# Causal zeroing on GpSimd instead of mask products on TensorE, with a retimed schedule, in an attention-and-mixture kernel

## The reference

```python
x = x + xattn(layernorm(x), ctx, ctx)        # 16 query heads, 4 key/value heads, width 32
    q, k = rope(rms_norm(q) ), rope(rms_norm(k))
    scores = q . k / sqrt(32); scores[key later than query] = -1e30
    out = softmax(scores) @ v @ w_out.T
x = x + ffn(layernorm(x))
    probs = softmax(x @ w_router); top 4 of 128 experts, weights normalised
    basis = silu(x @ w_gate[k]) * (x @ w_up[k])          # 8 shared bases of width 256
    out = sum over chosen experts of mix[expert] . basis @ w_down + shared expert
```

## Time and profile before

| | |
|---|---|
| median of 3 runs | 868.03 us (867.49 to 869.01) |
| the profiled execution | 869.35 us, its span 866.6 us |
| PE busy | 800.5 us, 92% |
| DVE, ACT, POOL busy | 650.2, 574.9, 493.8 us |

### The profile page before, as it was taken

One profiled execution on the slowest core, in us unless ns is written; L12 is line 12 of the kernel. 1 busy time (PEld: TensorE's weight loads), 2 busy tenths in 40 slices (PEclk: granted clock), 3 DMA queues, 4 the chain that ended last, 5 costly groups with the idle time before them and its releaser, 6 DMA issues.

```text
span 866.6 us, 15361 instructions
## 1 busy us (share of the span) xinstructions
PE 800.5 (92%) x4264; PEld 617.3 (71%) x4264; DVE 650.2 (75%) x1627; ACT 574.9 (66%) x1412; POOL 493.8 (57%) x682
## 2 busy tenths in 40 slices
PE   2668799999999999989999889989999999999998
PEld 1446567677776777768777668767777777877876
DVE  4736777788886767887888686878878875788774
ACT  1657877687776666778777575767787765554542
POOL 5457537894269526796278634797255512762461
PEclk9965999999999999999999999999999999999999
DMA  8031234544554245645445344454454443553650
GB/s 300 30 98 40 82 95 146 175 139 131 171 173 157 87 158 177 211 150 168 148 155 169 119 159 154 147 176 129 144 175 157 141 138 131 194 175 132 206 194 25
DMA packets 57795, 126.76 MB, mean 146 GB/s; under 512 B 12048, under 2 KB 28784, under 8 KB 57712
## 3 DMA queue, kind: packets, MB, share of 16 engines
q1 hardware_dynamic: 55888, 121.84, 42.8%
q10 hardware_dynamic: 1824, 3.94, 1.2%
HBM read 107.16 MB, written 4.19 MB: 128 GB/s over the span
## 4 chain that ended last, share of the span: by engine, by line
PE 67%; POOL 9%; DVE 6%; issue 6%; SPq 5%; ACT 3%; DMA 2%; POOLq 0%; DVEq 0%; ACTq 0%
PE u L1455 41%; PE u L1476 7%; PE o_bank L1371 3%; PE s L1331 3%; PE pair L1355 3%; SPq L557 2%; PE u L1439 2%; SPq L547 2%; POOL r_b L715 2%; DVE w_l L1102 1%; PE pair L1358 1%; POOL w_l L753 1%; PE s L1391 1%; DMA w_raw<-in_shared_w_down 1%; DMA w_raw<-in_w_units 1%
## 5 line engine op out<-in xcount | busy, mean ns | idle before, releaser
L1455 PE MATMUL u<-w_h,t_h 128*128 128x512 f32 x640 | 265.9, 415 | 8.4 <-POOL w_l L753 5.0
L1455 PE MATMUL u<-w_h,t_l 128*128 128x512 f32 x640 | 250.9, 392 | 0.0
L1455 PE MATMUL u<-w_l,t_h 128*128 128x512 f32 x640 | 250.8, 392 | 0.0
L1102 DVE TENSOR_TENSOR w_l<-w_raw,w_h 128x512 fp32r<-128x512 f32 x288 | 240.9, 864 | 0.0
L792 ACT ACTIVATE w_h<-w_raw 128x512 fp32r<-128x512 f32 x384 | 219.3, 622 | 27.1 <-DMA w_raw<-in_w_units 21.8
L753 POOL TENSOR_TENSOR w_l<-w_raw,w_h 128x512 fp32r<-128x512 f32 x96 | 135.4, 1410 | 101.5 <-ACT w_h L792 101.0
L827 ACT ACTIVATE scores<-scores,mx 128x384 f32<-128x384 f32 (+1 forms) x224 | 128.6, 575 | 62.0 <-DVE mx L1047 61.0
L1047 DVE CUSTOM_DVE_ANT_0 scores<-s,mask_qk 128x384 f32<-128x384 f32 (+1 forms) x224 | 112.5, 504 | 60.3 <-PE s L1331 59.4
L1455 PEld LDWEIGHTS u<-w_h,t_h 128*128 128x128 f32 x640 | 121.4, 190 | 37.3 <-issue 9.6
L761 POOL TENSOR_TENSOR macc<-macc,gb 128x256 f32<-128x256 f32 x112 | 104.2, 931 | 69.0 <-DVE gb L1203 68.7
L1455 PEld LDWEIGHTS u<-w_h,t_l 128*128 128x128 f32 x640 | 120.4, 188 | 27.2
(11 more groups left out here) (152 smaller groups left out, 1208.6 us busy)
## 6 DMA issues: line engine op xcount, KB each, us to landing
w_raw<-in_w_units SPq DMA_DIRECT2D x156, 512.0 KB, 4.2
w_raw<-in_shared_w_down SPq DMA_DIRECT2D x16, 512.0 KB, 4.6
q_st<-turned_h SPq DMA_DIRECT2D x232, 32.0 KB, 1.9
w_raw<-in_w_out_t SPq DMA_DIRECT2D x14, 512.0 KB, 3.8
out<-x SPq DMA_DIRECT2D x16, 256.0 KB, 2.5
q_st<-turned_l SPq DMA_DIRECT2D x116, 32.0 KB, 1.9
x<-in_x SPq DMA_DIRECT2D x3, 1024.0 KB, 7.0
w_raw<-in_w_units ACTq DMA_DIRECT2D x4, 512.0 KB, 11.8
```

Source lines behind the costliest of these rows:

```text
L1102: e.tensor_tensor(w_l[:, i % WR, k, :], w_raw[:, i % WR, k, :], f32(w_h[:, i % WR, k, :]), ALU.subtract).then_inc(s_wl, 1)
L1455: last = e.matmul(u_bank[n % 2][:], t[:, k, cols], ww[:, i % WR, k, :], start=(k == 0 and m == 0), stop=(k == KC - 1 and m == 2))
```

## The change

The 84 mask products and the tile `mask_kq` go. Instead POOL runs `mask_probabilities` one slot after the exponential (`SELECT = 1`): an `affine_select` in place on `pr` that writes zero where the key is later than the query, four heads by 128 queries in one instruction, 56 of them. For these tiles `value_products` waits for the select in place of the exponential.

`ones` moves from DVE (slot -11) to ACT, ahead of its slots. The first weights, which ACT issued, are issued by SP at slot -5, behind everything SP issues before. `rope_first` waits for the readers of its buffers rather than for the finished sum of the tile before (`cosined(n - 1)` and `s_rs` instead of `s_rope`); `rope_last` takes over the wait for `s_rope`. In the tables rope, spread, scales and moments of the start move by one to three slots, and within a slot the order changes on all engines: on PE the value products now stand before the long product's first half.

```diff
-LEAD = dict(inverse=-1, spread=1, second_pass=5, inverse_turn=4, values=9, high=0, rope=-11, turn=-1, stack=-1)
+LEAD = dict(inverse=-1, spread=2, second_pass=5, inverse_turn=5, values=9, high=0, rope=-14, turn=-1, stack=-3)
-PREP = dict(key_squares=(-39, 4, -29, -8), key_scale=(-40, 4, -28, -4), query_scale=(-36, 9, -22, 3), key_rope=(-33, 7, -21, 2),
-            key_turn=(-17, 13, -17, 5), key_stack=(1, 15, -16, 8))
+PREP = dict(key_squares=(-39, 4, -29, -8), key_scale=(-40, 3, -28, -3), query_scale=(-36, 9, -23, 3), key_rope=(-33, 5, -21, 2),
+            key_turn=(-16, 13, -17, 5), key_stack=(1, 15, -16, 8))
...
 def pass_b
-                    if k >= h * TH:
-                        last = e.matmul(dst[:, :, 0:P], ident16[:], mask_kq[:].unsqueeze(1).broadcast_to([P, n, P]),
-                                        start=False, stop=True, skip_group_check=True)
...
+            def mask_probabilities(u, k):
+                if u < KV or k < span(u)[1] * TH:
+                    return
+                n, w = step_no(u, k), Q - seen(u, k)
+                block = pr[:, n % PR, 0:G * w].rearrange("p (j q) -> p j q", j=G)[:, :, 0:P]
+                e.wait_ge(s_ex, n + 1)
+                e.affine_select(out=block, in_=block, compare_op=ALU.is_ge, fill=0.0, base=0,
+                                pattern=[[0, G], [1, P]], channel_multiplier=-1).then_inc(s_sel, 1)
...
 def value_products
-                    e.wait_ge(s_ex, n + 1)
+                    e.wait_ge(*probable(u, k))
...
 def rope_first
-                    e.wait_ge(s_rope, n)
+                    e.wait_ge(*cosined(n - 1))
+                    e.wait_ge(s_rs, n)
...
 vector_engine
-                e.memset(f32(k_st[MAXROW:ROWS, :, :]), 1.0).then_inc(s_ones, 1)
 scalar_engine
-            e.wait_ge(s_x0[1], 16)
-            load_chunk(e, 0)
...
+            e.wait_ge(s_mask, 1)
+            e.activation(k_st[MAXROW:ROWS, :, :], ident16[MAXROW:ROWS, 0:1].unsqueeze(2).broadcast_to([ROWS - MAXROW, KR, T]),
+                         ACT.Identity, scale=0.0, bias=1.0).then_inc(s_ones, 1)
```

More of the change, by code:

```diff
@@ L411, in last_span, with probable @@
             return c // KV * H * KV + KV + c % KV
+        def probable(u, k):
+            first = span(u)[1] * TH
+            if u < KV or k < first:
+                return s_ex, step_no(u, k) + 1
+            return s_sel, (u - KV) * TH + k - first + 1
         def second_pass_over(u):
@@ L595, in sync_engine @@
                     store(g)
-                if (u := of_query(s, "stack")) is not None and u >= U0:
-                    stack_queries(u)
+                for b in range(XR, B):
+                    if s == START[2 * (b - XR + 1)] + DOWN + XLOAD:
+                        load_x(b)
                 if s == LOADS[0]:
@@ L602, in sync_engine @@
                     load_x(2)
-                for b in range(XR, B):
-                    if s == START[2 * (b - XR + 1)] + DOWN + XLOAD:
-                        load_x(b)
+                if s == LOADS[2]:
+                    first_weights()
+                if (u := of_query(s, "stack")) is not None and u >= U0:
+                    stack_queries(u)
             for p in range(NT // 2):
@@ L765, in pool_engine @@
                     key_scale(hb)
+                if (step := second_pass_step(s - SELECT)) is not None:
+                    mask_probabilities(*step)
+                if (g := mixture(s, "scales")) is not None:
+                    norm_scale(g)
                 if (u := of_span(s, "spread")) is not None:
                     spread_inverse(u)
-                if (g := mixture(s, "scales")) is not None:
-                    norm_scale(g)
                 if (hb := of_half(s, "query_scale")) is not None:
@@ L955, in vector_engine @@
         def vector_engine(e):
-            def ones():
-                e.memset(f32(k_st[MAXROW:ROWS, :, :]), 1.0).then_inc(s_ones, 1)
             def key_squares(hb):
@@ L1251, in vector_engine @@
                     resident_low()
+                if s - 1 in fillers:
+                    evict[fillers[s - 1][0]](fillers[s - 1])
+                for u, m in first_pass_tiles(s)[1:]:
+                    row_max(u, m)
+                if (p := routing(s, "choose")) is not None:
+                    choose(p)
+                if (p := routing(s, "keep")) is not None:
+                    keep_largest(p)
+                if (g := mixture(s, "turn_x")) is not None:
+                    x_low(g)
                 if (g := turned_down(s)) is not None:
@@ L1266, in vector_engine @@
                     logits(g)
-                for n in range(U0 + 1):
-                    if s == ROPE3[n]:
-                        rope_stacked(n)
+                if (u := attended_in(s)) is not None:
+                    attended(u)
+                for g in moments_in(s):
+                    moments(g)
+                if (p := routing(s, "mix")) is not None:
+                    token_weights(p)
+                if (p := routing(s, "coefficients")) is not None:
+                    coefficients(p)
                 if (u := of_span(s, "inverse")) is not None:
@@ L1274, in vector_engine @@
                         weights_low(i, k)
-                if s == ONES:
-                    ones()
+                for n in range(U0 + 1):
+                    if s == ROPE3[n]:
+                        rope_stacked(n)
         def tensor_engine(e):
```

120 lines of the change are left out of this document (53 added, 67 removed).

## The result

The changed kernel takes 861.64 us in the median of 5 runs (856.14 to 863.66), the kernel before 868.04 on the same chip (5 runs, 867.49 to 869.06). The ratio is 0.9904, 95% interval 0.9878 to 0.993: 8.3 us faster by the ratio, 7.4 by the means and 6.4 by the medians of the runs just given; what follows goes by the ratios. The forecast was 856.0.

A forecast was written before the change was run, and what follows sets the result against it. PE was taken as the bound, with hand-overs bounding the start and POOL behind at batch switches. 869.35 - 16.1 - 4.0 + 8.1 = 857.35 us profiled, so 856.0 as median; own range 852 to 861, wide range 848 to 865.

The forecast's parts named there:

- POOL swallows most: Rival: selects at 1.17 us, longer DVE splits and a wait for ACT's exponential leave 861 to 866 us; chance 0.17.
- mask products removed: PE's second-pass steps: 28 spans save 0.26 for two masks and 0.32 for one wide mask, taken as -16.1 us.
- start and order in the slots: Start: earlier PE and shorter waits, -4.0 us at slot 14; reordering within slots: 4 either way allowed, taken as nothing.
- selects added: POOL: 56 selects of 0.8 us cost where POOL is behind, mainly three batch switches and the first two selects; +8.1 us.
- PE's idle time grows by what it saves: Rival: the saving on PE is filled by other waits, time within 1.7 us of 868; chance 0.05.
- PE's wait for POOL's split: Batch switches: two selects ahead of POOL's second weight split lengthen PE's wait for it by about 1.6 us.
- the slower rival: Each span: value products wait for the select; at 0.9 us a span, 873 us as a median; chance 0.09.
- The 2.1 for the memset: Start: without DVE's memset of `ones`, PE starts at 23.6 instead of 27.13 us, counted as -2.1.
- The 1.28 of the table load: Start: with weights on SP's queue and `ones` first on ACT, ACT's table load is over early, -1.28 us.
- the clock stays up in the start: Rival: the clock does not fall from 50 to 84 us, giving 5 us, 851; chance 0.19 shared with better order.
- The rule that was weighed: DVE and GpSimd exclude each other on SBUF: DVE splits 6 us longer, 0.4 us of the span, at most all 6.

The follow-up runs named there:

- experiment 2: The changed kernel with the mask products put back and the selects taken out: 862.1 us, ratio 0.9931 to the kernel before.
- experiment 3: The changed kernel with no causal mask in the second pass, neither selects nor mask products: 855.27 us, ratio 0.9844 to the kernel before.
- Experiment 1: The kernel before with only the mask products out and the selects in, its order of work kept: 867.73 us, ratio 0.9992.
- experiment 10: The changed kernel without any mask, with VectorE's split of the maxima issued earlier: 854.0 us, ratio 0.9815 to the kernel before.
- experiment 6: The changed kernel with PE's mask products kept for spans 4, 8, 16 and 24 and selects for the other 24: 858.42 us, ratio 0.9869.
- experiment 5: The changed kernel with the write of the ones back on VectorE at slot -11: 862.4 us, ratio 0.992 to the kernel before.
- experiment 12: The kernel before with each of its mask products issued twice: 876.15 us, ratio 1.0074.
- experiments 7 and 8: TensorE's turn of the maxima moved later in its slot, in the changed kernel (889.03 us, ratio 1.0236) and without masks (887.51 us, 1.0218).

## Why the prediction was right and where it was wrong

The direction and the wide range (848 to 865) held, and the removal stayed the largest term. The time missed by 5.6 us. At 861.6 it lies just outside the forecast's own range (852 to 861), in the one given to "POOL swallows most" (0.17), but not for that rival's reason: the selects cost less than forecast. Term by term, by ratios:

| term | predicted | measured |
|---|---|---|
| mask products removed | -16.1 | -7.5 (experiments 2, 3) |
| start and order in the slots | -4.0 | -6.0 (experiment 2) |
| selects added | +8.1 | +5.2 (3 against the changed kernel) |
| sum | -12.0 | -8.3 |

**The step that failed is "Mask products removed", taken as -16.1.** Two things were wrong in it. The wide mask was sized at 0.32 us by a step that no trace held, "0.69 less one product spacing" = 0.46. Experiment 1, in the same order of work, has this step: 0.56 in the median, from 0.78. The wide mask is thus worth 0.23, the pair 0.26 or 0.27: 13.7 us in place of 16.2. Then the sum took each distance on PE to the end, since PE was busy 97% of the middle. Of 13.7 us 7.5 arrived. The largest part of the rest is the wait for the split maxima, 4.8 us more in experiment 3 than in 2; moved out of the way in experiment 10 it gave 2.5 us by the ratios, inside the noise (4.6 by the profiled spans). The prediction named such waiting as "PE's idle time grows by what it saves", gave it 0.05 as a whole case, and never asked which wait would be the next. It could have: the row "PE s L1311 <- DVE mhl L1058: 2.0, 5, 0.7" stood in the waits of before, so there were places where PE already ran ahead of VectorE, and what is taken off PE right ahead of them is lost. The other part that the traces show is the clock, some 1 us on the mean and 4.3 in the profiled pair; the prediction had it only as a rival for the start.

**Selects.** The duration was right (0.8 predicted, 0.73 in the mean, 0.624 the least). Of the 8.1 us 2.2 were no cost of the selects but PE's own saving taken back (0.58 at each of three switches, and 0.5); without them the forecast is 5.9 for a measured 5.2, and the removal's is 13.9 for 7.5, so the failed step is the removal all the more. The place was right in part: products at the switches and at the first span give back 3.0 us (experiment 6, with an interval of some 3), net of what the four spans of products cost. The path was another one. PE's wait for POOL's split did not grow by 1.6 at the switches (4.5 us in 5 places in all, before 5.0 in 4); PE waits for the select itself, 1.54 and 1.07 us, at two switches of three. Of the slower rival, value products that wait in each span, these 2.6 us are all there is; the slot between select and values hides it elsewhere, as argued. Doubling the selects adds the same again, so POOL is not at an edge beyond which it swallows everything.

**The start.** PE's start is 2.05 us earlier, not 3.3. The 2.1 for the memset are right: experiment 5 gives 2.1 back at 27 and at 52 us. The 1.28 of the table load is where it failed: ACT's first output comes 0.8 us earlier (14.57 for 15.38), its third only 0.44 (22.10 for 22.54), since VectorE now waits 1.67 us for POOL's tile ahead of its copy at 18.64. The next such wait, 1.73 at 22.65, then sets PE's start; before, the memset lay over it. From slot 14 to 36 the kernel was 2.7 to 4.1 us ahead all the same, the -4.0 of the forecast. That the part alone gives 6.0 at the end leaves some 2 us to the order in the slots, which no row had priced; they were not separated by a run. One effect of the order is seen in the steps: the one with a single `pair` product takes 0.70 in the new order where it took 0.78, with its mask in both (experiment 2 against before), over 28 spans 2.2 us.

**The clock.** The rival "the clock stays up in the start" came in part: 0.61 for 0.51 from 50 to 84 us, by 27.3 us at the lower level for 34.1. But of the stretches that begin from 84 to 120 the kernel after has 13.6 us and the one before 3.4, and at 97 us it lost 2.5 of its 4.1 us behind a wait of 2.67 for a maximum. The five runs differ by 7.5 us, with a mean clock from 0.966 to 0.981, the fastest at the highest.

**The rule that was weighed.** POOL holds VectorE's instructions, as the trace of experiment 3 shows to 0.03 us. The Trainium skill (SBUF — State Buffer, "Who interferes with whom") says that the one that comes second is blocked for the whole instruction of the first, and that `tensor_scalar` can be concerned with a single input as well; the trace agrees with both (1.18 us for 0.17). As a price of the selects it was small: VectorE is busy 1.9 us more in the changed kernel than in experiment 3 (654.4 for 652.5), so 6 us were too many, and the 0.4 at the end cannot be told from nothing. The rule's weight lay elsewhere: not on the long splits that were looked at but on two small instructions with PE right behind them, and by GpSimd work that was there before.

Open: which part of the 6.0 us is order; why only 6.4 of 11.6 us arrive in experiment 12; and what experiment 10 owes to the earlier split and what to the removal. The accounts by product rest on one profile of each kernel.

## What to carry to other kernels

Price a removed instruction by the distance of starts, and then look in the waits for the engine that the freed one already waits for now and then: that row, however small, names where a part of the saving may be lost. It does not say how much: 2.0 us of it before became 6.6 without masks. On an engine that is behind at a few known places, keep the old form there and the new one elsewhere; here four spans of 28 gave back some 3 of 5 us, at the edge of the noise. Before an instruction is moved on the engine that waits, look at the queue of the engine that receives its result: a later place in PE's slot cost 29 us, with ACT's waits for it up by 45.

## What the hardware showed unexpectedly

The hold between VectorE and GpSimd goes both ways. Of the 56 selects 42 take 0.62 to 0.65 us; the other 14 take 0.75 to 1.20, and each of these ends 0.49 to 0.51 us behind the end of one of VectorE's weight splits.

The mean granted clock differs between kernels and between runs of one. Taking the time at the lower level as 2 x (1 - mean clock) x span, over the 148 runs of these 14 kernels for which the clock is known a run was 0.20 us (standard error 0.02) longer for each us more at the lower level than its kernel's mean. By kernel the mean was 43.0 us before, 46.4 after, 51.4 and 53.4 with selects in the old order and with two, and 39.3 and 39.8 with doubled and with restored mask products. But less work on PE is not what brings it on: the two kernels without any mask have 42.1 and 41.3, and the highest, 61.0 and 66.5, are experiments 7 and 8. What brings a single stretch on was not settled.
